# Part of the expert rounds between the cross attention steps of a decoder layer, with fp32r scores on half the rows

## The reference

```python
# linear attention, 8 heads of 64
q = softmax(x @ Wq, over a head's 64) * 64**-0.5
k = softmax(x @ Wk, over the tokens)
out = (q @ (k.T @ (x @ Wv))) @ Wo + bo
# cross attention on 1601 keys, 16 heads of 16
scores = (x @ Wq + bq) @ (ctx @ Wk + bk).T / 4
out = softmax(scores) @ (ctx @ Wv + bv) @ Wo + bo
# experts: 16 networks 256 -> 128 -> 256, 4 chosen per token, and a shared one
probs = softmax(x @ gate_w.T)
combine = the 4 largest of probs, divided by their sum, 0 elsewhere
act[e] = silu(x @ w1[e].T) * (x @ w3[e].T)
out = sum_e combine[e] * (act[e] @ w2[e].T) + shared(x)
```

## Time and profile before

| | us |
|---|---|
| median of 3 runs | 1275.68 (1275.11 to 1279.91) |
| the profiled execution's own time | 1280.25 |
| its span, first to last instruction | 1278.4 |
| TensorE busy in the span | 1177.9 |
| VectorE | 925.0 |
| ScalarE | 628.3 |
| GpSimd | 107.4 |

### The profile page before, as it was taken

One profiled execution on the slowest core, in us unless ns is written; L12 is line 12 of the kernel. 1 busy time (PEld: TensorE's weight loads), 2 busy tenths in 40 slices (PEclk: granted clock), 3 DMA queues, 4 the chain that ended last, 5 costly groups with the idle time before them and its releaser, 6 DMA issues. The chain is left out here.

```text
span 1278.4 us, 16160 instructions
## 1 busy us (share of the span) xinstructions
PE 1177.9 (92%) x5844; PEld 579.3 (45%) x5844; DVE 925.0 (72%) x1830; ACT 628.3 (49%) x1141; POOL 107.4 (8%) x94
## 2 busy tenths in 40 slices
PE   6993887799999999999999999999989989999996
PEld 3471555422323333333333332333227768888885
DVE  1317786697888878788887888878427767677675
ACT  1210222105777776777767777677783432322222
POOL 1213011500000000000000000000013410000000
PEclk9997898857999999999999999999999989999998
DMA  8000962102000000000000000000004411212120
GB/s 294 1 1 33 139 73 74 50 0 62 14 13 2 13 14 13 1 14 13 14 8 7 14 14 14 1 2 1 1 4 153 132 50 59 83 50 83 51 83 17
DMA packets 43055, 53.13 MB, mean 42 GB/s; under 512 B 4864, under 2 KB 31168, under 8 KB 42720
## 3 DMA queue, kind: packets, MB, share of 16 engines
q1 hardware_dynamic: 39104, 48.55, 14.4%
q10 hardware_dynamic: 3872, 3.56, 0.9%
HBM read 44.06 MB, written 7.83 MB: 41 GB/s over the span
## 5 line engine op out<-in xcount | busy, mean ns | idle before, releaser
L1084 DVE TENSOR_REDUCE mpart<-psum 128x1 f32<-128x400 f32 (+1 forms) x1024 | 522.9, 567 | 105.8 <-PE psum L733 101.4
L538 ACT ACTIVATE region<-psum 128x512 f32<-128x512 f32 (+1 forms) x832 | 450.2, 598 | 183.5 <-PE psum L755 182.3
L733 PE MATMUL psum<-region 96*128 96x400 bf16 (+1 forms) x1024 | 308.8, 352 | 8.7 <-DVE mpart L1084 5.6
L755 PE MATMUL psum<-region 99*128 99x512 bf16 (+1 forms) x832 | 285.0, 386 | 12.6 <-DMA region<-maxT 9.7
L766 PE MATMUL psum<-region 128*32 128x512 f32 (+1 forms) x1664 | 223.4, 609 | 0.7 <-ACT region L538 0.7
L755 PEld LDWEIGHTS psum<-region 99*128 99x128 bf16 (+1 forms) x832 | 80.6, 100 | 236.1 <-ACT region L538 186.8
L733 PEld LDWEIGHTS psum<-region 96*128 96x128 bf16 x1024 | 101.3, 99 | 181.2 <-DVE mpart L1084 132.8
L582 ACT ACTIVATE act_hi<-act_h 128x512 fp32r<-128x512 f32 x68 | 43.0, 632 | 176.0 <-DVE act_h L1260 176.0
L902 PE MATMUL psum<-x_hi,w_hi 128*128 128x512 f32 x272 | 109.9, 404 | 1.9 <-POOL w_lo L405 1.9
L903 PE MATMUL psum<-x_lo,w_hi 128*128 128x512 f32 x272 | 108.0, 397 | 0.0
L904 PE MATMUL psum<-x_hi,w_lo 128*128 128x512 f32 x272 | 108.0, 397 | 0.0
(11 more groups left out here) (148 smaller groups left out, 1027.0 us busy)
## 6 DMA issues: line engine op xcount, KB each, us to landing
blend_a<-gates_d SPq DMA_DIRECT2D x32, 256.0 KB, 3.2
blend_b<-gates_d SPq DMA_DIRECT2D x32, 256.0 KB, 3.2
region<-qparts_d SPq DMA_DIRECT2D x96, 64.0 KB, 2.2
region<-kparts_d SPq DMA_DIRECT2D x6, 800.5 KB, 28.0
qparts_d<-region SPq DMA_DIRECT2D x4, 768.0 KB, 3.5
kparts_d<-region SPq DMA_DIRECT2D x3, 800.5 KB, 5.3
xT<-in_xT SPq DMA_DIRECT2D x1, 2048.0 KB, 8.9
x_sb<-in_x ACTq DMA_DIRECT2D x1, 2048.0 KB, 24.1
```

The source lines that it names most:

```text
L538: act.activation(prob[0:r, s % 3, j, :], bank(n % ST_BANKS)[0:r], ACT.Exp).then_inc(p_ready, 1)
L733: pe.matmul(bank(MAX_BANKS[u % len(MAX_BANKS)])[:, 0:w], qstack[0:SROWS, buffer(G), j, qt * P:(qt + 1) * P], kstack[0:SROWS, g * GROUP + j ...
L755: pe.matmul(bank(n % ST_BANKS)[0:r], kstack[0:SROWS + LEVELS, g * GROUP + j, kt * P:kt * P + r], qstack[0:SROWS + LEVELS, buffer(G), j, :] ...
L1084: dve.tensor_reduce(mpart[:, u // UNITS % 2, v // PIECES, v % PIECES:v % PIECES + 1], bank(MAX_BANKS[u % len(MAX_BANKS)])[:, 0:w], X, ALU. ...
```

## The change

Keys and queries are cut into two fp32r parts and three products instead of six, 48 rows. The even heads of a pair lie on partitions 0 to 63, the odd ones on 64 to 127 (`SIDES`). A max unit is one token tile, a pair of heads and 512 keys, in two banks, read by one reduce; the 65 keys left (66 columns are taken) make two units for all four tiles of a group. 26 units make a group, two a step, 17 steps ahead. `weigh` runs two steps behind.

From step 67 (`FIRST_PIECE`) to 192, each step also holds one part of an expert round: the first inner products, the outer products of the round before, or the second inner products. So 42 rounds (`IN_STEPS`) lie in the steps and 26 behind them. One bank (`H_BANK`) serves both inner products, two (6 and 7) the outer ones, one the numerators. The scores then have a ring of two banks, and the max units one pair. The transposes and projections take turns in the same ring (`EXTRA`), and ScalarE copies each out of it.

The weights are cut once, by GpSimd, during the linear attention, written to memory (`wsplit_d`), and fetched for each round. The gates are made for each chunk and not for three chunks at once. The product and the remainder of a round are made by VectorE in the steps as well as behind them.

```diff
-SPLIT = 6
-LEVELS = 3
+SPLIT = 3
+LEVELS = 2
...
-PIECES = 4
-UNITS = TPC * GROUP * PIECES
-LEAD = KT + 3
+SIDES = 2
+HALF = P // SIDES
+PAIRS = GROUP // SIDES
+MAIN = KEYS // CHUNK
+UNITS = TPC * PAIRS * MAIN + PAIRS
+PER_STEP = UNITS // KT
+LEAD = KT + 4
+IN_STEPS = 42
+FIRST_PIECE = KT * GROUPS + KT + 2
+W_SLOTS = 2
+TAIL_SLOTS = 8
...
+        def ring_bank(n):
+            return n % 3 if n < NARROW else (n - NARROW) % 2
+        def unit_bank(u):
+            return (4, 6)[u % 2] if u < SINGLE else 4
+        def unit_free(u):
+            return u - 1 if u < SINGLE else u
...
     # SyncE
+            load_raw(0)
+            for e in range(FFN):
+                if e + 1 < FFN:
+                    load_raw(e + 1)
+                store_split(e)
...
+                r, part = piece(s)
+                if part == "out" and r >= 1 and r + 1 < IN_STEPS:
+                    load_weights(r + 1)
+                if part == "second":
+                    rc, e = network(r)
+                    if e < EXPERTS and e + B_SLOTS < EXPERTS:
+                        load_blend(EXPERTS * rc + e + B_SLOTS)
...
     # GpSimd
+            for e in range(FFN):
+                pool.wait_ge(ld_raw[e % 2], 16 * 3 * (e // 2 + 1))
+                if e >= 2:
+                    pool.wait_ge(split_written[e % 2], 16 * (e // 2))
+                link(pool.tensor_copy(w_stage[:, e % 2, 0, :], w_raw[e % 2]))
+                pool.tensor_tensor(w_stage[:, e % 2, 1, :], w_raw[e % 2], w_stage[:, e % 2, 0, :].bitcast(F32),
+                                   ALU.subtract).then_inc(raw_split, 1)
...
-            pool.memset(region1[SROWS:SROWS + LEVELS, 0:KW], 1.0 + 0x3F80 * 2.0 ** -23).then_inc(zeros_ready, 1)
+            pool.memset(kstack[:, :, :].bitcast(F32), 1.0).then_inc(zeros_ready, 1)
...
     # VectorE
-                link(dve.tensor_scalar(kf[:, f, :], kf[:, f, :], C_SCALE, None, ALU.mult))
-                link(dve.tensor_copy(kpart[:, 0, f, :], kf[:, f, :]))
-                link(dve.tensor_tensor(kres, kf[:, f, :], kpart[:, 0, f, :], ALU.subtract))
-                link(dve.tensor_copy(kpart[:, 1, f, :], kres))
-                link(dve.tensor_tensor(kres, kres, kpart[:, 1, f, :], ALU.subtract))
-                ins = dve.tensor_copy(kpart[:, 2, f, :], kres)
+                link(dve.tensor_scalar(kpart[:, 0, f, :], kf[:, f, :], C_SCALE, None, ALU.mult))
+                ins = dve.scalar_tensor_tensor(out=kpart[:, 1, f, :], in0=kf[:, f, :], scalar=C_SCALE,
+                                               in1=kpart[:, 0, f, :].bitcast(F32), op0=ALU.mult, op1=ALU.subtract)
...
+                for u in range(units_until(s - 1), units_until(s)):
+                    read_max(u)
...
+                r, part = piece(s)
+                if part == "first":
+                    if r >= 1:
+                        second_part_act(r - 1)
+                    silu(r)
+                if part == "second":
+                    weigh_inner(r)
+                    product(r)
...
     # ScalarE, within the four exponentials of a step
+                    if j == 2:
+                        if kt == 1 and G >= 1:
+                            copy_num(G - 1)
+                        r, part = piece(s)
+                        if part == "first":
+                            if r >= 1:
+                                first_part_act(r - 1)
+                            tanh(r)
...
     # TensorE
+                for at, t in enumerate(tiles):
+                    for side in range(SIDES):
+                        rows_of = slice(HALF * side, HALF * side + SROWS)
+                        mm = pe.matmul(bank(unit_bank(u) + side)[:, at * w:(at + 1) * w],
+                                       qstack[rows_of, buffer(G), p, t * P:(t + 1) * P],
+                                       kstack[rows_of, g * PAIRS + p, keys], start=True, stop=True)
...
+                p, side = divmod(j, SIDES)
+                rows = slice(HALF * side, HALF * side + SROWS + 1)
+                pe.matmul(ring(n)[0:r], kstack[rows, g * PAIRS + p, kt * P:kt * P + r],
+                          qstack[rows, buffer(G), p, :], start=True, stop=True).then_inc(ring_full, 1)
...
+            def part_of_round(s):
+                r, part = piece(s)
+                if part == "first":
+                    if r == 0:
+                        pe.wait_ge(ring_read, NARROW)
+                    else:
+                        pe.wait_ge(weighted_ready, r)
+                    inner(r, 0, bank(H_BANK))
+                if part == "out" and r >= 1:
+                    outer(r - 1)
+                if part == "second":
+                    pe.wait_ge(silu_ready, r + 1)
+                    inner(r, 1, bank(H_BANK))
...
+                if s >= 2:
+                    weigh(s - 2)
+                scores(s, 0)
+                if s >= FIRST_PIECE:
+                    scores(s, 1)
+                for u in units[0:1]:
+                    max_unit(u)
+                part_of_round(s)
+                if s < FIRST_PIECE:
+                    scores(s, 1)
+                scores(s, 2)
+                if s >= FIRST_PIECE:
+                    scores(s, 3)
+                for u in units[1:]:
+                    max_unit(u)
+                if s < FIRST_PIECE:
+                    scores(s, 3)
+                behind_scores(s)
```

More of the change, by code:

```diff
@@ L61, in buffer @@
     return (G + 1) % GROUPS
-def piece(n):
-    at = 0 if n == 0 else PW + (n - 1) * (PW - 1)
-    return at, PW if n == 0 else PW - 1
-assert sum(piece(n)[1] for n in range(PIECES)) == KEYS and LASTK > 0
+assert LASTK > 0 and REST * TPC <= CHUNK and UNITS == PER_STEP * KT
 def decoder_layer(nc, a, out):
@@ L550, in _ @@
[L550 to L558 removed]
+                act.activation(attnT[:, k, :], ring(n), ACT.Copy).then_inc(ring_read, 1)
```

1235 lines of the change are left out of this document (710 added, 525 removed).

## The result

The changed kernel takes 1285.77 us (median of 14 runs, 1279.28 to 1289.26) against 1276.02 (14 runs of the kernel before on the same chip): a ratio of 1.0065, 95% interval 1.0049 to 1.0081. The forecast was 1188. The change is slower, by a little, and clear of the noise.

A forecast was written before the change was run, and what follows sets the result against it. The prediction saw TensorE nearly full before the change and VectorE bounding most attention steps after it. Its terms, 236 + 37 + 176 + 560 + 45 + 137, gave a 1191 us span, so 1188 us, range 1160 to 1225.

The forecast's parts named there:

- Narrow scores, a pair at 0.24 us: Score and max matmuls: two heads on separate row tiles run at once, 0.24 us a pair, against 0.47 one after the other.
- Steps 0 to 66, 2.45 us: Attention steps without rounds: VectorE bounds them at 2.3 us plus 0.15 for coupling; 176 us with 12 for row work and divisions.
- A mixed round, 12.2 us: Steps 67 to 192, three steps per round: VectorE's reads, round operations and waits set 12.2 us; TensorE needs 11.0.
- Row work, 50 us, bounds 20 and 90: Residuals, norms, gates and outputs in the mixed steps: taken as twice today's 25 us, since it also lies on VectorE's path.
- The prediction is wrong if row work costs over 90 us: Stated failure sign for row work in the mixed steps; the other sign was a pair over 0.4 us.
- The last 15 steps, 3.0 us: Steps behind the last max units: two score banks make S2 wait for S0's exponential, 3.0 us against 2.40, 45 us in all.
- Before the steps and the rounds left over: Start: first max at 236 us instead of 253.3; behind the steps: 26 rounds, tail and end, 137 us.
- serial sides: Rival on the score and max pairs: two sides run one after the other, 0.47 us a pair, 1296 us; chance 0.18.
- Waits in the narrow rings: Rival on the mixed steps: narrow rings and in-order round work cost 0.5 us more a step, 63 us, 1251; chance 0.20.

The follow-up runs named there:

- e3_one_side: Changed kernel with both heads of each pair computed from the same rows, so their matmuls cannot overlap: 1486.5 us in the fastest of four executions, 1511 to 1534 in the others.
- y2_half_reads: Changed kernel with VectorE reading only 256 of each max bank's 512 scores in the lead-in and steps 0 to 66: 1272.9 us, ratio 0.9967.
- x7_pool_rest: Kernel with rounds begun at step 82, with GpSimd instead of VectorE making the remainders of the rounds in the steps: 1242.9 us, ratio 0.9727.
- e4_split_reads: Changed kernel with VectorE reading and freeing a max unit's two banks separately in the mixed steps: 1289.3 us, ratio 1.0103.
- y1_fewer_matmuls: Kernel with rounds begun at step 82, with 12 instead of 18 matmuls in each round in the steps: 1208.8 us, ratio 0.9477.
- x5_no_choice: Changed kernel with the choice of the four experts left out of VectorE's work in all four chunks: 1273.9 us, ratio 0.9956.
- x3_filler: Changed kernel with six more idle 512-column fp32r matmuls a step in the last 14 steps: 1271.3 us, ratio 0.9954.
- x6_fewer: Kernel with rounds begun at step 82, with 38 instead of 42 rounds in the steps, begun at step 94: 1240.2 us, ratio 0.9710.
- c8_mid: Kernel with rounds begun at step 82 and the choice spread over eight steps, with the product between second and third score in steps 0 to 81: 1220.2 us, ratio 0.9559.
- e2_weigh_late: Changed kernel with the product placed behind the last max unit in steps 0 to 66: 1309.2 us, ratio 1.0229.

## Why the prediction was wrong

The steps that failed are the bound of the plain steps, the price of row work and the clock of the last steps. Point by point, by its own parts:

- *Narrow scores, a pair at 0.24 us.* The mechanism was right: row tiles overlap, in the traces and by e3_one_side.
- *Steps 0 to 66, 2.45 us "VectorE bounds it".* This failed: +15 us of the +29.5, by 67 x 0.22. VectorE does not bound it (y2_half_reads). TensorE's order with the ring of three does: first score, its exponential, fourth score, product, 0.59 + 0.60 + 0.05 + 0.43 + 0.99 us. The sum put TensorE at 2.1 us, as if the fourth score could pair with a max matmul; it waits for its bank and runs alone. No place of the product removed the wait wholly (2.67, 2.83 and 2.61 us at three places). The other 15 us are turns and chunk 0's row work, for which the sum had 12 and the trace has 27, part of it at a fallen clock.
- *A mixed round, 12.2 us.* The number came out by luck, for the reason did not. "VectorE's chain sets the time" is out: less VectorE work changes next to nothing (x7_pool_rest), filled gaps neither (e4_split_reads), and less TensorE work does (y1_fewer_matmuls). TensorE's own work is 3 x 3.91 = 11.7 us by the step shown, where the sum had 11.0: a change of tiling costs 0.1 us on either side of it, and the sum had one side. How the last half microsecond divides between score banks and the pair of max banks is open.
- *Row work, 50 us, bounds 20 and 90.* The largest miss: 610 - 500 - 10 = 100 us. Twice the old price was a choice, not a reading. By the repeats of the steps it has two parts. 13 mixed steps with their two turns take 56.6 us where 13 plain ones would take 52.9: 3.7 us a group, 36 us in 9.7 groups. The five groups that also hold a chunk's row work take 64.4, 71.3, 65.2, 70.9 and 71.2 us, 60 us more than 5 x 56.6; the two parts make 96 of the 100. Of the 60, 14 us are the choice of the experts: it holds VectorE for 4 us, and with one pair of max banks TensorE stands behind it (x5_no_choice). The group of 71.3 us shows most of the rest: TensorE waits some 0.55 us for ScalarE ahead of every bank of row work, and then does the bank's own matmuls, in all about 1.1 us for a transposed one and about 2.3 for the gates' logits and for each half of a projection. Once it waits 1.87 us for the max banks, whose read stands behind the layer norm on VectorE. Two lines of it, the matmuls of a projection's bank and the max pair behind the wait of 1.87 us:

```profile
671.42 1.97 PE L1044 MATMUL psum<-wo_c,attnT 128*128 128x256 f32 x8 [0.54 <-ACT region L795]
```

```profile
689.54 0.50 PE L978 MATMUL psum<-kstack,qstack 48*128 48x512 f32 x2 [1.87 <-DVE mpart L1405]
```

  Other than the choice, no run takes one of these out alone. The forecast's own sign, "The prediction is wrong if row work costs over 90 us", names this step.
- *The last 15 steps, 3.0 us.* Two steps took 3.16 and 3.13, so the chain was read rightly (its four terms as written add to 2.6; the fourth score's own 0.4 to 0.5 us is missing among them). Then the clock fell and each step took 4.61, +22 us. x3_filler shows it: work that nobody needs brings 3.69. The forecast gave the clock no term behind the lead-in, though it rested on steps that would leave TensorE with less to do than the earlier trace rows.
- *Before the steps and the rounds left over.* Right within 8 and 3 us. GpSimd's splitting ended at 111.4 us (93 to 111 said) and the tile loop began at 123.3 (125 said); two of VectorE's four operations on the keys took 1.5 us longer beside GpSimd's than alone (2.50 and 3.31 us against 0.99 and 1.83), as the forecast had allowed; the other 6 us were won between there and the first maximum.

The rivals: serial sides are out. "Waits in the narrow rings", 0.5 us a step more, had the sign but not the place: plain mixed steps came as forecast, and the price sits at row work, where every bank brings its wait of 0.55 us. None of the cases held that TensorE would be the bound everywhere and that its clock would fall.

Where did the gain go that was to come from rounds in idle time? There was none to fill. Three mixed steps less three plain ones are 12.2 - 8.0 = 4.2 us, a round's 4.19 of the earlier trace rows, and x6_fewer shows the two to be of one price. The narrower scores gave 0.3 us a step, the time up to the first score 28 us (293.7 to 265.5), and row work, the first mixed steps and the last 15 steps took it all back. Rounds pay only where TensorE would otherwise have too little to do: in the last steps. With the rounds moved there, the choice spread and the product placed anew (c8_mid), the same change is worth 56 us.

## What to carry to other kernels

Before moving work into another stage, subtract: the price of a step with the work less that of a step without it, against the price of the work alone. If the receiving stage's fullest engine is also the work's, nothing is gained, and what else lives there (turns, small serial jobs) costs more once buffers are fewer. Put moved work where the engine runs short of it, above all at a stage's end, and check the granted clock of what remains.

## What the runs showed of the hardware

- Six more matmuls of 512 columns a step made 14 steps faster, 3.69 against 4.61 us, for the granted clock stood at 1.00 instead of 0.50.
- The clock also fell to half while the trace has TensorE busy throughout (160.00 of 160 us at 0.53 in e3_one_side, 37.10 of 37.10 us at 0.50 in steps 2 to 9 of e2_weigh_late). Whether it is granted does not follow from the busy share of the trace.
- Four column tiles of 32 columns take 0.99 us together, and two of them 0.98.
- Two row tiles of 48 and 49 rows share their time fully inside a stream of pairs, at 0.23 us a pair of 512 columns. Next to matmuls of another tiling a pair costs 0.33, against 0.57 to 0.58 on one row tile (e3_one_side).
- A change of tiling between fp32r matmuls costs 0.1 us on either side of it: the last one before it and the first one behind it are each followed after 0.33 us instead of 0.23.
- TensorE takes matmuls of the two row tiles out of the queue's order. In steps 2 to 61 of the changed kernel that hold two full max units (55 of them), the max matmul that starts within 0.01 us of the first score is the one that carries the unit's semaphore increment, by the code the second of its pair, on the rows that the score leaves free; the first one starts 0.33 us later. VectorE's read still begins only when both have ended (303.55 in the step shown). In e3_one_side, where all are on the same rows, the order is kept.
